# Starting expert 0 inside the drain of the attention pipeline: four early slots, unrolled experts, and a split shared with GpSimd

## The chip, the core and the metric

The kernel runs on one core of one Trainium2 chip, in one launch. The metric is the device time in microseconds (us). The kernel before takes 1063.76 us (median of 3 runs, 1062.62 to 1063.82).

A core has five engines with a queue of instructions each: TensorE (PE, matrix products into the PSUM banks), VectorE (DVE), ScalarE (ACT), GpSimd (POOL) and SyncE (SP, which issues most transfers). They meet only at semaphores. Transfers run on 16 shared DMA engines.

## The reference, cut to what matters

```python
x = layernorm(x + retention(x))                    # 32 sequences of 128 tokens, 256 channels
x = layernorm(x + cross_attention(x, ctx))         # causal, 16 heads
logits = x @ router_w.T                            # 8 experts, top 2 of them per token
h = gelu(x_e @ w_fc[e] + b_fc[e])                  # 256 -> 1024, expert by expert
y_e = h @ w_proj[e] + b_proj[e]                    # 1024 -> 256
x = layernorm(x + sum of y_e * share_e)
```

## The kernel before, in words

**Attention stage.** The 32 sequences go through a software pipeline. `step(k)` exists once on each engine and works on parts of the sequences k+1 to k-4: retention for k, the row maxima of attention for k-1, its values for k-2, second norm and router logits for k-3, top 2 and the place of each row for k-4. An engine takes these parts in the order in which the code writes them. `pick` finds the top 2, `put` counts and gives each token its row in the region of its expert, and on GpSimd `shares` works out the two weights of a token and `send` scatters its two rows into `sent_rows` in DRAM by indirect DMA. `filled` holds the next free row of each region.

**Drain.** After step 31 only the late parts are left. `step_drained` runs them on TensorE, with three filler products (`idle`, L625) ahead of each. When the last `put` is done, a chain of small VectorE instructions (L1112 to L1127) makes the table `tab_i`: slots per expert and the number of the first one. TensorE runs 64 filler products (`CHANGE_IDLE`) meanwhile.

**Expert stage.** The rows of an expert are taken in slots of 256. For each slot SP loads the rows, TensorE turns them (`turn_rows`, L673), ScalarE and VectorE make a high part and a low part of them (`xs_hi`, `xs_lo`), and TensorE runs 8 pieces `fc(j)` of 6 products (L699) and 8 pieces `proj(j)` of 6 products (L710); `proj` runs three pieces behind `fc`. For each piece ScalarE computes GELU twice (`h_hi` L903, `h_f` L909), and VectorE the difference `h_lo` (L1158). GpSimd adds the two halves of the weighted result to `residual_sum` (L1306). In the first slot of each expert the weights of the next are split as well: ScalarE makes seven of the eight high parts (`split_hi`, L837) and VectorE the eighth (`last_hi`, L1057) and all eight low parts (`split_lo`, L1062). Two sets of split weights take turns; `w_raw` is one buffer, loaded again (2 MB, L330 and L333) when `raw_split` says that it has been split.

Each engine runs the experts as a loop over three pairs and two more bodies written out. At the head of each body it loads the number of slots and the number of the first slot from `tab_i` into registers.

**Split of expert 0.** It is done in steps 28 to 31 (`SPLIT`, `SPLITS`), two of eight pieces a step.

**Last stage.** 8 blocks of 512 tokens are loaded, normalized and stored.

## Time and profile before

| | |
|---|---|
| median of 3 runs | 1063.76 us |
| profiled execution: its time, its span | 1062.52 us, 1060.7 us |
| steps 2 to 31 of the attention stage | 16.17 us each up to step 27, then 17.2 us |
| last attention product `att_values(31)` to first expert product | 551.5 to 580.1 us |
| expert products, 36 slots | 580.1 to 1025.1 us |
| last loads, norm, stores | 1025.1 to 1060.7 us |
| busy | PE 92%, DVE 61%, ACT 55%, POOL 34% of the span |
| granted TensorE clock | 0.979 of full speed on average |

How to read it: the busy share of an engine is an average over stages that are bound in different ways. In the expert stage what matters is the distance between the starts of slots; in the attention stage the distance between the starts of steps; and between the two stages the chain of waits. A row of the chain has its start, its length, the engine, what it writes and the line. "issue" is time in which the engine waited for nothing that the profile shows.

### The profile page before, as it was taken

The numbers are of one execution on the slowest core, as the hardware profiler recorded it, in microseconds if no ns is written. First come the engines' busy times: TensorE is split into PE (matmuls) and PEld (weight loads), VectorE is DVE, ScalarE is ACT, GpSimd is POOL, SyncE is SP. The second block draws the span as 40 slices with busy tenths as digits, with TensorE's granted clock in tenths as the row PEclk, the third lists the DMA queues.
The fourth block names the chain that finished last, engine by engine and source line by source line (L and its number), as shares of the span: only waits on it lengthen the run. The fifth ranks groups of instructions, "written<-read, shape, count | busy, mean of one in ns | idle before, by whom it ended". The sixth has DMA issues, their size and how long they took to land.

```text
span 1060.7 us, 31797 instructions
## 1 busy us (share of the span) xinstructions
PE 979.8 (92%) x11554; PEld 876.7 (83%) x11560; DVE 641.8 (61%) x1951; ACT 588.5 (55%) x1565; POOL 359.1 (34%) x599
## 2 busy tenths in 40 slices
PE   6999999999999999999887999999999999999960
PEld 4778888888888888888654999999999899999960
DVE  3467676676776676767743645565464655564436
ACT  3455555555655555556531656565565665565534
POOL 1124443444444444444433122222323222223223
PEclk9899999999999999999999999999999999999985
DMA  6001231111111111110032144422525342522227
GB/s 235 32 24 50 87 137 52 62 42 51 62 37 57 47 47 63 41 37 33 16 120 76 32 95 84 120 49 41 138 40 137 84 86 40 129 43 48 45 36 316
DMA packets 55831, 78.73 MB, mean 74 GB/s; under 512 B 5616, under 2 KB 44784, under 8 KB 55472
## 3 DMA queue, kind: packets, MB, share of 16 engines
q1 hardware_dynamic: 39984, 57.45, 16.9%
q0 software_dynamic: 13536, 18.16, 9.9%
q10 hardware_dynamic: 2208, 1.73, 0.6%
q8 instruction: 67, 1.10, 0.4%
q14 instruction: 36, 0.29, 0.1%
HBM read 51.04 MB, written 28.66 MB: 75 GB/s over the span
## 4 chain that ended last, share of the span: by engine, by line
PE 66%; DVE 15%; issue 6%; ACT 4%; POOL 4%; DMA 3%; ACTq 1%; DVEq 0%; POOLq 0%; SPq 0%
PE bank L699 17%; PE bank L710 16%; DVE row_max L945 7%; PE bank L437 5%; PE bank L552 3%; PE bank L452 3%; PE bank L427 3%; PE bank L597 3%; PE bank L505 3%; PE bank L477 3%; ACT h_f L909 2%; PE bank L583 2%; PE bank L472 2%; POOL grstd L1238 2%; DVE x_pre L976 1%
## 5 line engine op out<-in xcount | busy, mean ns | idle before, releaser
L903 ACT ACTIVATE h_hi<-bank,bfc_s 128x256 fp32r<-128x256 f32 x288 | 140.1, 487 | 175.0 <-PE bank L699 171.0
L1306 POOL DMA_INDIRECT residual_sum<-y_w,meta_i x72 | 117.6, 1634 | 340.9 <-DVE y_w L1182 330.0
L1158 DVE TENSOR_TENSOR h_lo<-h_f,h_hi 128x256 fp32r<-128x256 f32 x288 | 122.6, 426 | 176.6 <-ACT h_f L909 156.9
L699 PE MATMUL bank<-xs_hi,w_hi 128*128 128x256 f32 x576 | 166.4, 289 | 16.5 <-DVE xs_lo L1140 9.4
L699 PE MATMUL bank<-xs_lo,w_hi 128*128 128x256 f32 x576 | 162.7, 282 | 0.0
L710 PE MATMUL bank<-w_hi,h_lo 128*128 128x256 f32 x576 | 162.6, 282 | 0.0
L710 PE MATMUL bank<-w_hi,h_hi 128*128 128x256 f32 x576 | 162.5, 282 | 0.0
L699 PE MATMUL bank<-xs_hi,w_lo 128*128 128x256 f32 x576 | 161.2, 280 | 0.0
L710 PE MATMUL bank<-w_lo,h_hi 128*128 128x256 f32 x576 | 161.0, 280 | 0.0
L909 ACT ACTIVATE h_f<-bank,bfc_s 128x256 f32<-128x256 f32 x288 | 140.1, 487 | 0.0
L699 PEld LDWEIGHTS bank<-xs_hi,w_hi 128*128 128x128 f32 x576 | 108.4, 188 | 19.5 <-issue 19.5
L710 PEld LDWEIGHTS bank<-w_hi,h_hi 128*128 128x128 f32 x576 | 108.3, 188 | 0.7
L699 PEld LDWEIGHTS bank<-xs_lo,w_hi 128*128 128x128 f32 x576 | 108.5, 188 | 0.0
L699 PEld LDWEIGHTS bank<-xs_hi,w_lo 128*128 128x128 f32 x576 | 108.3, 188 | 0.0
L710 PEld LDWEIGHTS bank<-w_lo,h_hi 128*128 128x128 f32 x576 | 108.3, 188 | 0.0
L710 PEld LDWEIGHTS bank<-w_hi,h_lo 128*128 128x128 f32 x576 | 108.2, 188 | 0.0
L805 ACT ACTIVATE att_p<-bank 128x512 f32<-128x512 f32 x128 | 69.2, 599 | 28.7 <-PE bank L561 28.7
L940 DVE TENSOR_TENSOR ret_p<-bank,decay 128x512 f32<-128x512 f32 x128 | 79.2, 681 | 7.9 <-PE bank L452 7.9
L945 DVE TENSOR_REDUCE row_max<-bank 128x4 f32<-128x512 f32 x128 | 78.9, 679 | 2.5 <-PE bank L530 2.5
L1269 POOL DMA_INDIRECT sent_rows<-x_row,pos x64 | 64.3, 1005 | 18.3 <-issue 14.5
L415 PE MATMUL bank<-xcT,wqk_s 128*128 128x128 f32 x512 | 65.6, 281 | 0.8 <-DMA wqk_s<-in_w_qkv 0.8
L415 PEld LDWEIGHTS bank<-xcT,wqk_s 128*128 128x128 f32 x512 | 59.6, 191 | 7.0 <-issue 5.8
(170 smaller groups left out, 1985.1 us busy)
## 6 DMA issues: line engine op xcount, KB each, us to landing
rows<-sent_rows SPq DMA_DIRECT2D x37, 258.0 KB
xcT<-in_turned SPq DMA_DIRECT2D x32, 256.0 KB, 2.9
w_raw<-in_w_fc SPq DMA_DIRECT2D x8, 1024.0 KB
w_raw<-in_w_proj SPq DMA_DIRECT2D x8, 1024.0 KB
x_t<-in_x SPq DMA_DIRECT2D x32, 128.0 KB, 2.7
residual_sum<-x_row SPq DMA_DIRECT2D x32, 128.0 KB, 1.8
last_in<-residual_sum SPq DMA_DIRECT2D x8, 512.0 KB, 7.5
result<-last_out SPq DMA_DIRECT2D x8, 512.0 KB, 2.7
```

The source lines that it names most:

```text
L415: last = mm(ps_prep[:, m * P:(m + 1) * P], wqk_s[:, k, m * P:(m + 1) * P], xcT[c.r][:, 0, k, :], start=(k == 0), stop=(k == NCH - 1))
L437: last = mm(ps_prep[:, i * C:(i + 1) * C], xcT[c.r][:, i, k, :], w[:, k, :], start=(k == 0), stop=(k == NCH - 1))
L699: last = mm(ps_h[j % 4][:, 0:SLOT], w[:, at:at + P], v[:, k, :], start=(n == 0), stop=(n == 3 * NCH - 1))
L710: last = mm(ps_out[half][:, 0:C], v[j % 4][:, cols], w[:, at:at + C], start=(j == 0 and n == 0), stop=(j == HC - 1 and n == 2))
L805: A(att_p[:, r, :], ps_s[r][:, :], ACT.Exp, scale=SCALE).then_inc(s["att_exp"], 1)
L903: A(h_hi[j % 4][:, :], ps_h[j % 4][:, 0:SLOT], ACT.Gelu_apprx_tanh, bias=bias)
L909: A(h_f[j % 2][:, :], ps_h[j % 4][:, 0:SLOT], ACT.Gelu_apprx_tanh, bias=bias)\
L940: V.tensor_tensor(ret_p[:, r, :], ps_s[r][:, :], decay[:, r, :], ALU.mult)\
L945: V.reduce_max(row_max[:, r, 0:HPT], ps_s[r][:, :].rearrange("p (h s) -> p h s", s=T), AX.X)\
L1158: V.tensor_tensor(h_lo[j % 4][:, :], h_f[j % 2][:, :], h_hi[j % 4][:, :].bitcast(f32), ALU.subtract).then_inc(s["h_split"], 1)
L1269: G.indirect_dma_start(sent_flat, bass.IndirectOffsetOnAxis(pos[c.r][:, k:k + 1], 0), x2_row[c.r][k][:, :], None).then_inc(s_sent[c.r], 16)
L1306: G.indirect_dma_start(total, bass.IndirectOffsetOnAxis(meta_i[:, half:half + 1], 0), y_w[:, half, :], None, compute_op=ALU.add)\
```

## The change

1. **Early slots.** The first 27 sequences (`EARLY_SEQ`) send their rows for expert 0 to the first rows of `sent_rows`; 4 slots (`EARLY`) of 256 rows of it are computed straight behind `att_values(31)`. The remaining parts of the drain (`rank_out`, `rank_last`, `last_norms`, `last_places`, `copies_last`) and the table are written between the pieces of slots 0 and 1. `put` sets the counter of expert 0 to at least 1024 after sequence 26, so that the region behind holds the rest. These 1024 rows are filled with padding at the very start, by four transfers on SP's queue that GpSimd waits for (`early_padded`) before its first work.
2. **Experts written out.** `experts` is a Python loop over 8 experts with fixed numbers. Each engine loads the 8 slot counts once, TensorE in slot 2 and ScalarE and VectorE in slot 3, and adds registers after that.
3. **GpSimd's share.** `ON_POOL = (1, 3, 5)`: three of eight low parts of the next weights are made by GpSimd. VectorE still waits for all eight (`w_ready`) at the end of the first slot.
4. **Split of expert 0** in steps 21 to 28, one piece a step, and the load of the weights of expert 1 from step 29.
5. **`gap_exp`** leaves ScalarE. GpSimd computes the exponential as a power, as the first link of `shares`.
6. The two halves of the result share one PSUM bank; `rows` goes to another bank. `CHANGE_IDLE` and the advance load of the GELU table (L880) are gone.

```diff
-SPLIT = B - 4
-SPLITS = 2
+SPLIT = B - 11
+SPLITS = 1
-CHANGE_IDLE = 64
+EARLY = 4
+EARLY_SEQ = 27
+ON_POOL = (1, 3, 5)
...
-            with eng.Fori(0, E // 2 - 1) as pair:
-                for k in range(2):
-                    body(2 * pair + k, k, True, True)
-            body(E - 2, 0, True, False)
-            body(E - 1, 1, False, False)
+            g = EARLY
+            for e in range(E):
+                body(e, e % 2, slots[e], g, e + 1 < E, e + 2 < E)
+                g = g + slots[e]
...
+                if k == B - 1:                      # SP
+                    for r in range(4):
+                        sp.wait_ge(s_sent[r], 32 * len(range(r, EARLY_SEQ, 4)))
+                    early_rows(0)
                 run(store_total, At(k - 3))
+                if k == 0:
+                    for g in range(EARLY):
+                        sp.dma_start(sent_flat[g * SLOT:(g + 1) * SLOT, :].rearrange("(h p) c -> p h c", p=P),
+                                     pad_row).then_inc(s["early_padded"], 16)
...
+            def rank_out(j):                        # TensorE, beside slot 0
+                if j == 0:
+                    logits(At(B - 2))
+                if j == 1:
+                    o_turn(At(B - 1))
+                if j == 3:
+                    att_back(At(B - 1))
+                if j == 4:
+                    att_proj(At(B - 1))
+                    rank(At(B - 2))
+                if j == 8:
+                    x2_turn(At(B - 1))
+                if j == 10:
+                    logits(At(B - 1))
...
+            slot(0, 0, rank_out)
+            slot(1, 0, rank_last)
+            slot(2, 0, count_next)
+            for g in range(3, EARLY):
+                slot(g, 0)
...
-            act.wait_ge(s["gap_exp"], B)
-            A(gelu_warm[:, :], half_neg[:, 0:1], ACT.Gelu_apprx_tanh)
+            def copies_last(j):                     # ScalarE, beside slot 0
+                if j == 3:
+                    att_back_out(At(B - 1))
+                if j == 6:
+                    x2_T_out(At(B - 1))
+                    x2_again(At(B - 1))
...
+            def last_norms(j):                      # VectorE, beside slot 0
+                if j == 0:
+                    lg_out(At(B - 2))
+                if j == 1:
+                    att_norm(At(B - 1))
+                if j == 2:
+                    pick(At(B - 2))
+                if j == 4:
+                    ln2_stats(At(B - 1))
+                    put(At(B - 2))
+                if j == 5:
+                    ln2_norm(At(B - 1))
...
-                pool.wait_ge(s["gap_exp"], c.n + 1)
+                pool.wait_ge(s["gap_done"], c.n + 1)
+                ch.link(G.tensor_tensor(gap_e[:, :], base_e, gap[:, :], ALU.pow))
...
+            pool.wait_ge(s["early_padded"], 16 * EARLY)
             for half in range(HALVES):
                 G.dma_start(total[N_TOK + half * P:N_TOK + (half + 1) * P, :], pad_row[:, half, 0:C])
+            slots = []
+            steps(step)
+            drain()
...
+                if has_next:                        # GpSimd, head of each expert
+                    for j in ON_POOL:
+                        split_lo(e + 1, 1 - par, j)
```

What the edits do to the order of the queues, at four places.

TensorE between the stages, before: L625 is filler, L605 `x2_turn`, L611 `logits`, L619 and L620 `rank`, L673 `turn_rows` of the first slot.

```order
L620 MATMUL bank<-hot_b,bits 128x8
L625 MATMUL bank<-bits 128x512 x3
L605 MATMUL bank<-small,x_row_0 128x128 x2
L625 MATMUL bank<-bits 128x512 x3
L611 MATMUL bank<-rt_s,x2T 128x8 x2
L625 MATMUL bank<-bits 128x512 x3
L619 MATMUL bank<-hot_b,bits 128x8
L620 MATMUL bank<-hot_b,bits 128x8
L625 MATMUL bank<-bits 128x512 x64
L673 MATMUL bank<-small,rows 128x128 x4
```

After, in the same place: L605 is now `att_values(31)`, L704 `fc`, L643 `logits`, L615 `o_turn`, L657 filler.

```order
L637 MATMUL bank<-small,x_row_0 128x128 x2
L657 MATMUL bank<-bits 128x512 x3
L605 MATMUL bank<-att_p,v_att 32x128 x16
L704 MATMUL bank<-xs_hi,w_hi 128x256
L704 MATMUL bank<-xs_lo,w_hi 128x256
L704 MATMUL bank<-xs_hi,w_lo 128x256
L704 MATMUL bank<-xs_hi,w_hi 128x256
L704 MATMUL bank<-xs_lo,w_hi 128x256
L704 MATMUL bank<-xs_hi,w_lo 128x256
L643 MATMUL bank<-rt_s,x2T 128x8 x2
L704 MATMUL bank<-xs_hi,w_hi 128x256
L704 MATMUL bank<-xs_lo,w_hi 128x256
L704 MATMUL bank<-xs_hi,w_lo 128x256
L704 MATMUL bank<-xs_hi,w_hi 128x256
L704 MATMUL bank<-xs_lo,w_hi 128x256
L704 MATMUL bank<-xs_hi,w_lo 128x256
L615 MATMUL bank<-small,att_o 128x128 x4
L704 MATMUL bank<-xs_hi,w_hi 128x256
```

The first product of expert 0 stands directly behind the last product of attention, and the late parts of the drain stand between its pieces. The 64 filler products are gone.

ScalarE in the same place, before: L829 is `gap_exp`, L823 `x2_again`, L880 the advance load of the GELU table, L889 `xs_high(0)`.

```order
L818 ACTIVATE x2T<-bank 128x256 [waits x2_T]
L829 ACTIVATE gap_e<-gap 128x1 [waits shared,gap_done]
L823 ACTIVATE x_row_1<-x_row_0 128x256 [waits x2_done]
L829 ACTIVATE gap_e<-gap 128x1 [waits shared,gap_done]
L880 ACT_TABLE_LOAD
L880 ACTIVATE gelu_warm<-small 128x1 [waits gap_exp]
L889 ACTIVATE xs_hi<-bank 128x512 [waits consts_expert,tab_ready,rows_turned]
```

After: L888 is `att_exp(31)`, L901 `x2_T_out`, L892 `o_out`, L906 `x2_again`, L962 and L968 the two GELU outputs of slot 0.

```order
L888 ACTIVATE att_p<-bank 128x512 [waits att_scores] x4
L901 ACTIVATE x2T<-bank 128x256 [waits x2_T]
L892 ACTIVATE att_o<-bank 128x512 [waits att_done]
L906 ACTIVATE x_row_1<-x_row_0 128x256 [waits x2_done]
L962 ACT_TABLE_LOAD [waits consts_expert,fc_done]
L962 ACTIVATE h_hi<-bank,bfc_s 128x256
L968 ACTIVATE h_f<-bank,bfc_s 128x256 [waits h_split]
```

The table for GELU is now loaded behind the wait for the first `fc` of slot 0 (`fc_done`), and `o_out(31)` and `x2_again(30)` stand ahead of it.

GpSimd at the start of the program, before: L1228 makes `xb` of sequence 0, L1235 to L1238 its `grstd`.

```order
L1220 UNCONDITIONAL_BRANCH [waits barrier_Pool_Activation_PE_DVE_SP_gather]
L1228 ISA
L1228 TENSOR_TENSOR xb<-x_t,gnb 128x256 [waits zeroed,got_late,loaded0,got_small,got_gn]
L1235 TENSOR_TENSOR gmsq<-gm 128x1 [waits gn_moments]
L1236 TENSOR_TENSOR gvar<-gm,gmsq 128x1 [waits gn_chain]
L1237 TENSOR_TENSOR gvar<-gvar,small 128x1 [waits gn_chain]
L1238 TENSOR_TENSOR grstd<-gvar,small 128x1 [waits gn_chain]
```

After: L1476 fills the padding rows behind `residual_sum` (formerly L1288, at the end of the attention stage), L1375 makes `xb`.

```order
L1367 UNCONDITIONAL_BRANCH [waits barrier_Pool_Activation_PE_DVE_SP_gather]
L1476 DMA residual_sum<-in_small_c 128x256 [waits zeroed,got_late,early_padded,got_small,got_gn]
L1476 DMA residual_sum<-in_small_c 128x256
L1375 ISA
L1375 TENSOR_TENSOR xb<-x_t,gnb 128x256 [waits loaded0]
L1382 TENSOR_TENSOR gmsq<-gm 128x1 [waits gn_moments]
L1383 TENSOR_TENSOR gvar<-gm,gmsq 128x1 [waits gn_chain]
L1384 TENSOR_TENSOR gvar<-gvar,small 128x1 [waits gn_chain]
L1385 TENSOR_TENSOR grstd<-gvar,small 128x1 [waits gn_chain]
```

Two transfers and the wait for `early_padded` stand ahead of the first `xb` now.

SyncE after, at the end of expert 0: L398 is the loop over slots, L403 loads rows, L337 and L340 load the weights of expert 2, L299 and L300 pad the region of expert 2.

```order
L398 UNCONDITIONAL_BRANCH
L398 ISA
L403 ISA
L403 DMA rows<-sent_rows 128x2x258
L398 REGISTER_ALU
L398 COMPARE_AND_BRANCH
L337 DMA w_raw<-in_w_fc 128x2x1024
L340 DMA w_raw<-in_w_proj 128x8x256
L299 TENSOR_LOAD tab_i
L299 ISA x2
L300 ISA
L300 DMA sent_rows<-in_small_c 128x2x258
L398 UNCONDITIONAL_BRANCH
L398 ISA
L403 ISA
L403 DMA rows<-sent_rows 128x2x258
```

The order of these transfers is that of before; but the first loop now runs twice for expert 0 instead of six times, so the rows of expert 1's first slot stand behind the weights of expert 2 one slot after these are asked for.

## Rows read from the trace of the kernel before

**Rows 1.** Chain of waits, slots (start, length, engine, tile, line, count).

```profile
605.48 2.84 PE bank L699 x24
...
617.29 2.84 PE bank L699 x24
...
653.67 1.00 PE bank L699 x6
...
667.02 3.12 PE bank L699 x24
...
673.69 0.44 PE bank L673 x4
```

**Rows 2.** Chain of waits, attention steps and last split.

```profile
460.87 1.73 PE bank L437 x8
...
477.04 1.73 PE bank L437 x8
...
494.25 1.73 PE bank L437 x8
...
528.27 1.04 ACT w_hi L837 x2
```

**Rows 3.** Windows (length, PE, PEld, DVE, ACT, POOL busy, clock, DMA share, GB/s).

```profile
530.00:534.00 4.00, 4.00 (x20) 3.36 (x23) 1.95 (x11) 0.55 (x2) 1.52 (x2) 0.51 0.20 70
```

**Rows 4.** Chain of waits, from attention to the first expert.

```profile
550.47 1.01 PE bank L573 x32
...
555.57 0.97 PE bank L597 x4
...
560.10 0.31 PE bank L605 x2
...
569.87 4.46 DMA sent_rows<-x_row,pos
...
580.06 2.42 PE bank L699 x18
```

**Rows 5.** Timeline of ScalarE at the change of stages.

```profile
562.95 1.28 ACT L880 ACT_TABLE_LOAD   x1
```

**Rows 6.** Waits of TensorE after 580 us.

```profile
PE bank L699 <- issue: 7.2, 7, 1.4
```

**Rows 7.** Timeline of GpSimd at the start.

```profile
20.50 0.72 POOL L1228 TENSOR_TENSOR xb<-x_t,gnb 128x256 f32<-128x256 f32 x1 [20.03 <-DMA rt_s<-in_router_t]
```

**Rows 8.** Windows at the start, and over a load of weights.

```profile
16.00:18.00 2.00, 2.00 (x35) 1.71 (x24) 0.04 (x1) 1.12 (x5) 0.00 (x0) 1.00 1.06 372
18.00:20.00 2.00, 2.00 (x18) 1.84 (x16) 0.61 (x2) 0.10 (x1) 0.00 (x0) 1.00 0.40 120
630.00:641.00 11.00, 11.00 (x96) 11.00 (x95) 4.94 (x14) 6.81 (x17) 3.31 (x2) 1.00 0.93 262
```

**Rows 9.** DMA issues of SyncE (KB each, us to landing).

```profile
sent_rows<-in_small_c SPq DMA_DIRECT2D x8, 258.0 KB, 8.1
```

**Rows 10.** GpSimd issues on `residual_sum` (ns min/median/max).

```profile
L1288 POOL DMA_DIRECT2D residual_sum<-in_small_c x2: 561/590/620, 570.8 to 571.4; - x2
```

**Rows 11.** Timeline of SyncE in the first slots.

```profile
630.01 0.37 SPq L330 DMA_DIRECT2D w_raw<-in_w_fc  x1
...
633.33 0.66 SPq L293 DMA_DIRECT2D sent_rows<-in_small_c  x1
```

**Rows 12.** Single lines of VectorE and GpSimd (ns min/median/max, first and last).

```profile
L976 DVE SCALAR_TENSOR_TENSOR x_pre<-y_c,grstd,xb x32: 484/485/485, 22.6 to 522.0; 128x256 f32<-128x256 f32 x32
...
L1238 POOL TENSOR_TENSOR grstd<-gvar,small x32: 548/561/567, 22.0 to 521.4; 128x1 f32<-128x1 f32 x32
...
L1246 POOL TENSOR_TENSOR x_row<-gap_s,small x32: 548/691/692, 82.7 to 566.2; 128x1 f32<-128x1 f32 x32
...
L1261 POOL TENSOR_TENSOR x_bo<-x,bo_s x32: 722/730/733, 25.2 to 527.9; 128x256 f32<-128x256 f32 x32
...
L1062 DVE TENSOR_TENSOR w_lo<-w_raw,w_hi x64: 681/693/761, 477.8 to 939.4; 128x512 fp32r<-128x512 f32 x64
```

More of the change, by code:

```diff
@@ L276, in steps @@
                 between()
-            for k in range(B + DRAIN):
+            for k in range(B):
                 step(k)
@@ L351, in _ @@
             steps(step)
+            for k in range(B, B + 3):
+                step(k)
             sp.wait_ge(s["counts_ready"], 1)
@@ L651, in step @@
                 run(o_turn, At(k - 2))
-            def step_drained(k):
-                for stage, back in ((att_back, 3), (att_proj, 3), (att_scores, 2), (rank, 4), (x2_turn, 3),
-                                    (att_values, 2), (logits, 3), (o_turn, 2)):
-                    if At(k - back).exists():
-                        idle(DRAIN_IDLE)
-                        stage(At(k - back))
             def between():
@@ L665, in _ @@
             idle(START_IDLE, y_sq[:, 0:TW * 2].bitcast(bf16), y_sq[:, :].bitcast(bf16))
-            steps(step, between)
             def turn_rows(g):
@@ L728, in _ @@
-            experts(pe, expert)
+                with pe.Fori(0, n_slots) as i:
+                    slot(before + i, par)
+            experts(expert, slots)
         @block.scalar
@@ new lines, in _, with expert @@
+            act.wait_ge(s["got_small"], 16)
+            steps(step, between)
+            drain()
+            act.wait_ge(s["consts_expert"], 16 * CONSTS_EXPERT)
+            act.sem_inc(s["h_done"], EVER)
+            slot(0, 0, None, copies_last)
+            for g in range(1, EARLY - 1):
+                slot(g, 0)
+            act.wait_ge(s["tab_ready"], 1)
+            slots = []
+            slot(EARLY - 1, 0, None, lambda j: slots.append(count(act, j)))
+            def expert(e, par, n_slots, before, has_next, has_after):
+                slot(before, e, (e + 1, 1 - par) if has_next else None)
@@ L917, in expert @@
                 with act.If(n_slots > 1):
                     with act.Fori(1, n_slots) as i:
-                        slot(before + i, False)
-            experts(act, expert)
+                        slot(before + i, e)
+            experts(expert, slots)
             for b in range(NLAST):
@@ new lines, in _, with expert @@
+            steps(step)
+            drain()
+            dve.wait_ge(s["consts_expert"], 16 * CONSTS_EXPERT)
+            slot(0, 0, None, last_norms)
+            slot(1, 0, None, last_places)
+            for g in range(2, EARLY - 1):
+                slot(g, 0)
+            dve.wait_ge(s["tab_ready"], 1)
+            slots = []
+            slot(EARLY - 1, 0, None, lambda j: slots.append(count(dve, j)))
+            def expert(e, par, n_slots, before, has_next, has_after):
+                slot(before, e, (e + 1, 1 - par) if has_next else None)
@@ L1186, in expert @@
                 with dve.If(n_slots > 1):
                     with dve.Fori(1, n_slots) as i:
-                        slot(before + i, False)
-            experts(dve, expert)
+                        slot(before + i, e)
+            experts(expert, slots)
             def last_stats(b):
@@ L1289, in _ @@
                     .then_inc(s_added[half], 16 * EVER)
+            slots = []
+            steps(step)
+            drain()
             for r in range(4):
```

474 lines of the change are left out of this document (284 added, 190 removed).

## The prediction, made before the changed kernel was run

> **What bounds the kernel now.** I read the chain of waits first, because it says for each stage which engine's end is waited for. In the expert stage it is TensorE: a plain slot runs from 605.48 to 617.29, 11.81 us of products [rows 1]. The first slot of an expert takes 667.02 - 653.67 = 13.35 us, since ScalarE and VectorE also split the next weights there and the next slot's low part comes late [rows 1]. At each of the 7 changes of expert TensorE waits about 1 us more for nothing but its own register loads: 7.2 us in all [rows 6]. In the attention stage a step takes 477.04 - 460.87 = 16.17 us, and 494.25 - 477.04 = 17.21 us where expert 0's weights are split [rows 2]. Its period is not TensorE's work but a loop: products, `grstd` on GpSimd, `x_pre` on VectorE, the row maxima, products again. Between the stages the reader is to see a long chain in which TensorE has nothing but filler: attention's last product ends at 550.47 + 1.01 = 551.48, then come the projection, the norm and the turn (560.10), the last send lands (569.87 + 4.46), and the first expert product starts at 580.06 [rows 4]. That is 28.6 us.
>
> **The sum, part by part**, against the profiled execution (1062.52 us; the median of the runs is 1.2 above it).
>
> *Handover, -28.6.* The number of slots stays: by the inputs expert 0 gets 1300 rows, 1094 of them from the first 27 sequences, so 4 early slots are full and 2 follow; 6 before, 4 + 2 after. So the whole of 551.48 to 580.06 goes, and what was computed in it comes back inside slots 0 and 1.
>
> *What stands before the first GELU, +1.1.* In the order of after `o_out(31)` and `x2_again(30)` stand ahead of slot 0 on ScalarE. `x2_again` takes some 0.4 us and `o_out` is waited for behind `att_values(31)`; I take 1.1 for the start of the GELU chain.
>
> *Slot 0, +7.0.* Products that moved in: two logits, `o_turn`, `att_back`, `att_proj` (555.57), one `rank`, `x2_turn` (0.31 us [rows 4]), some 3.3 us, an estimate from the lengths of such products. Stalls: the GELU table (1.28 us [rows 5]) is now loaded behind the wait for the first `fc`, so it lies on the path; `o_turn`, `rank` and `proj(7)` each wait for a piece of VectorE or ScalarE that is queued behind the GELUs and differences of the slot, together about 2.5. So 3.3 + 1.3 + 2.4 = 7.0. From below 4.6 (only products and table); from above 12, if each of the five late parts (turn, back, projection, norm, turn) waits its own way through two busy engines, at 1 to 2 us each.
>
> *Slots 1 and 2, +1.4.* One `rank` and a table of 2.6 us of VectorE, which has slack in a plain slot (its own busy share is under half, 4.94 of 11 us [rows 8]): +0.4. Slot 2 has the 8 register loads on TensorE: one change of expert costs 1.0 for two loads and the branch [rows 6]; eight loads spread over pieces, +1.0 (0 to 4).
>
> *The drain's first part, -2.0.* The chain has 1.04 us of ScalarE's split in step 31 [rows 2], which is gone, and behind it the clock dips: 0.51 of full speed, half of the 2.4 GHz, from 530 to 534, when TensorE had waited for that split [rows 3]. I take 1.0 of the dip's 2 us.
>
> *The split spread, -2.2.* Four steps of two pieces cost 4 x (17.21 - 16.17) = 4.2. Now eight steps have one piece: ScalarE and VectorE each have one less operation of 0.7 us [rows 12] in the loop's slack, which I put at 0.25 a step: 2.0 instead of 4.2 (0 to 4.2).
>
> *Experts written out, -3.2.* Seven waits of 1.0 [rows 6]; the loop branch inside an expert stays and one jump remains, about 0.5 each: 7.2 to 4.0 (0.7 to 7).
>
> *The start, +5.5.* This is the added wait with the largest price. GpSimd's queue now begins with the wait for four transfers of 258 KB, and behind that wait stand two transfers of its own and then `xb(0)`; `x_pre(0)` on VectorE waits for `xb(0)`, and the whole pipeline behind it. Before, `xb(0)` started at 20.50, held by the last constant that it needs [rows 7]. In this stretch the DMA engines are full: share 1.06 from 16 to 18 us and 0.40 from 18 to 20 [rows 8]; so the pads can't be moved beside the constants, only behind them. One costs, by 2882 KB in 11 us at share 0.93 [rows 8], 258 / 282 = 0.9 us of all engines, say 1.1; four, 4.4. They finish at about 18.8 + 4.4 + 1.5 of landing = 24.7, and GpSimd issues its two transfers at 0.59 us each [rows 10]: `xb(0)` starts at 25.9, +5.4. From below 1.2 (the two issues only, the pads fully hidden); from above 9, a pad by itself takes 8.1 us from issue to landing [rows 9].
>
> *Expert 0 with two slots, +6.0.* SyncE's queue has, in order, the rows of slot 5, the weights of expert 2 (2 MB), the pad of expert 2, the rows of slot 6 (the order of after). The weights wait for the split of the raw ones, done about 12.5 us into slot 4. Before, expert 0 had six slots, and this load was issued at 630.01 beside its fifth [rows 11], its pad 3.3 us later; nothing waited. Now the rows of slot 6 are issued about 15 us after slot 4's start, behind 2 MB and 258 KB on the same queue: at 262 GB/s [rows 8] 2048 + 258 KB are 9 us, so they land near 25.5. TensorE needs them for `turn_rows(6)` in slot 5, at 673.69 - 653.67 = 20.0 [rows 1]. The stall is 5.5 us, and a wait of this length may cost the clock that rows 3 show, 0.5 more. From below 0 (rows pass beside the weights), from above 8 (with the full dip).
>
> *GpSimd's three low parts, +2.0.* A GpSimd operation on 128x256 takes 0.73, the VectorE one on 128x512 0.69 [rows 12]; so one piece on GpSimd is an estimated 1.45. VectorE is relieved of 3 x 0.69, but at the end of a first slot it is late because ScalarE's last GELU is late, not for its own work; no gain. The wait that this adds: VectorE waits for all eight parts (`w_ready`) at j = 7, and behind that stand the low part of the next rows, for which TensorE waits, and the bias. GpSimd should be done about 2 us before. I put +0.3 for each of 7 experts for operations side by side (0 to 0.6 each: `x_row` takes 0.548 at least and 0.691 in the median [rows 12], so operations on these two engines do stretch one another).
>
> *`gap_exp`.* GpSimd's power is the first link of `shares`; as a 128x1 operation with a power it costs 0.56 like `grstd` [rows 12], on an engine with 34% of work, and its chain has a whole step. +0.2 with the rest.
>
> Sum: -28.6 + 1.1 + 7.0 + 1.4 - 2.0 - 2.2 - 3.2 + 5.4 + 6.0 + 2.0 + 0.2 = -12.9. 1062.5 - 12.9 = 1049.6; with half of the 1.2 to the median, **1050**.
>
> **The rivals.**
>
> *A. The two added queues cost nothing* (the start 1.2 instead of 5.4, the rows of slot 6 not late): 1050 - 4.2 - 6.0 = 1040, and less with a smaller slot 0. For it: the DMA engines are idle from 20 to 22 us, and the transfers have 16 engines. Against: both stand in one queue in order, and the wait on GpSimd is ahead of all its work. Chance 0.15.
>
> *B. Slot 0 is much longer* (12 instead of 7), because five late parts follow each other through engines that also do GELU: 1055 to 1058. For it: the same chain took from 551.5 to 569.9 when these engines were free [rows 4]. Against: slot 1 takes part of it. Chance 0.10.
>
> *C. The loop of the steps grows: slower than before.* Its place is between `grstd` and `x_pre`. `pow` of `gap` is the next thing in GpSimd's queue behind `grstd`, reads SBUF, lasts 0.56 us, and `x_pre` (484 ns, two SBUF inputs, on the loop) starts 0.04 to 0.08 us after `grstd` ends. If an operation of GpSimd that holds SBUF keeps VectorE out to its end, `x_pre` starts up to 0.5 us late in 28 steps: 14 us, and each of the three low parts costs VectorE 0.6 instead of 0.3 per expert (+2). That gives 1050 + 14 + 2 = 1066. It decides the sign from (1063.8 - 1050 - 2) / 28 = 0.42 us a step. Against it: `gap_s` of GpSimd stands beside `x_pre` now, and `x_pre` is 484 to 485 ns in all 32 steps; what is longer is GpSimd's `x_row`, 0.69 against 0.55 [rows 12]. So GpSimd seems to be the one held, at least where VectorE comes first. Chance 0.07.
>
> The Trainium skill ("SBUF — State Buffer", section "Who interferes with whom") has this rule: a VectorE instruction with two SBUF inputs contends with a GpSimd instruction that reads SBUF, through a shared pair of ports which whoever issues first holds for the whole instruction. By that rule case C is how it would go, since `pow` issues first; the trace agrees with it in that `x_row` is longer beside `x_pre`, and has no row in which a long GpSimd operation came first.
>
> *D. The change doesn't do what it says:* the 27 sequences do not fill 1024 rows, and a slot of padding (+11.8) is computed. 1094 against 1024: chance 0.01.
>
> **How the numbers follow.** The forecast (1044 to 1056) has 0.65, A 0.15, B 0.10, C 0.07, D and the rest 0.03. The range 1039 to 1058 takes in A and most of B, and leaves C, D and the far ends of the bounds, some 0.15. About 0.2% or 2.1 us is what a measurement of this kernel can tell from no change: faster needs 1061.6 or less. That holds for the forecast, A and B: 0.90. Same 0.03, slower (C, and D with B) 0.07.
>
> **What the profile after would show.** Right, if: `xb(0)` starts near 26; steps are still 16.2 apart up to the first split and 16.4 in steps 21 to 28; the first `fc` stands directly behind `att_values(31)`; slot 0 lasts 19; the GELU table load is on the chain inside it; `turn_rows(6)` waits some 5 us for a transfer; the issue wait at changes of expert halves; first slots stay 13.4 to 13.7. Wrong, if `x_pre` starts 0.3 us or more behind `grstd`, if `xb(0)` starts before 23 or after 29, if slot 0 exceeds 24, or if VectorE waits for GpSimd at `w_ready`.

## The result, and the profile after

The changed kernel takes 1058.44 us (median of 14 runs) against 1063.28 us of the kernel before: ratio of 0.9958, 95% interval 0.9945 to 0.9972. It is faster by 4.8 us; 1050 was forecast, with a range of 1039 to 1058. One of the 14 runs, of 1116.65 us at a granted clock of 0.924, was in a slower state of the chip and is not in the ratio.

The chain of waits of the changed kernel has these rows at the start and at the change of stages (start, length, engine, tile, line, count); they answer to [rows 1, 2, 4 and 7].

```profile
12.19 12.41 DMA sent_rows<-in_small_c
...
25.28 1.37 POOL residual_sum L1476 x2
26.75 0.74 POOL xb L1375
...
28.86 0.49 DVE x_pre L1077
```

```profile
530.08 0.50 DVE x_pre L1077
...
556.56 1.06 PE bank L605 x32
557.80 0.95 PE bank L704 x6
...
631.41 7.55 DMA rows<-sent_rows
639.00 0.66 PE bank L690 x4
...
644.64 0.72 PE bank L704 x6
...
659.40 3.13 PE bank L704 x24
```


The first rows are the added wait: the last of SyncE's pads lands at 24.6, two transfers of GpSimd follow, and `xb(0)` starts at 26.75. In the second block `att_values(31)` ends at 557.6 and the first expert product starts 0.2 us later: the gap of 28.6 us is gone. But at 631.41 a load of rows takes 7.55 us, and the first slot of expert 1, from 644.64 to 659.40, lasts 14.8 us (13.35 in the kernel before).

TensorE's waits in the expert stage (line waited with, releaser: us in total, times, longest), as [rows 6]:

```profile
PE bank L717 <- DVE h_lo L1248: 11.5, 8, 1.5
PE bank L704 <- DVE xs_lo L1218: 7.6, 7, 1.1
PE bank L690 <- DMA rows<-sent_rows: 3.2, 1, 3.2
PE bank L615 <- DVE lg L1125: 1.9, 1, 1.9
```


The 7.2 us of issue are no longer there. In their place stand 11.5 us for `h_lo`, a wait that the kernel before did not have.

Where the time went, from the starts of `x_pre` (L976, now L1077) of each step and of `xs_lo` (L1140, now L1218) of each slot, in both traces. A plain slot is 11.81.

| stretch | before | after | difference | forecast |
|---|---|---|---|---|
| `x_pre(0)` starts | 22.59 | 28.86 | +6.3 | +5.4 |
| steps 0 and 1 | 27.47 | 28.36 | +0.9 | 0 |
| steps 2 to 30 (split) | 471.97 | 472.86 | +0.9 | -2.2 |
| `x_pre(31)` to the end of attention | 29.45 | 27.53 | -1.9 | -2.0 |
| to the first expert product | 28.58 | 0.19 | -28.4 | -28.6 |
| slots 0 to 3, beyond plain slots | | | +9.6 | +9.5 |
| second slot behind the early ones | | 14.97 | +3.4 | +6.0 |
| changes of expert | 7.2 | 0 | -7.2 | -3.2 |
| 7 first slots | 97.0 | 107.3 | +10.3 | +2.0 |
| 15 other slots of odd experts | 11.81 | 11.95 | +2.0 | 0 |
| last stage | 37.00 | 37.26 | +0.3 | 0 |

The 97.0 are the sum of the first slots before (103.2) without the six waits of about 1.03 us at their start. The rows give -3.8; the spans differ by -4.1. The rows of the start hold some scatter: seven traces with the same code up to step 3 have `x_pre(0)` at 27.8 to 28.9 and 26.8 to 28.4 us for steps 0 and 1. Slots 0 to 3: from the first product to `xs_lo(1)` 19.26, in a plain slot 10.45, so +8.8; then +0.6, +0.3, -0.1.

### The profile page after: what moved, and what is told of

The parts are those of the page before. It is cut to its first block, busy times and chain, and to the rows that moved or that the text cites. A ratio compares the mean times of both kernels' runs of the same rounds, so it can differ in the third digit from the quotient of the medians.

```text
span 1056.6 us, 31053 instructions
## 1 busy us (share of the span) xinstructions
PE 965.9 (91%) x11474; PEld 873.5 (83%) x11474; DVE 648.2 (61%) x1931; ACT 587.5 (56%) x1531; POOL 399.0 (38%) x651
## 4 chain that ended last, share of the span: by engine, by line
PE 67%; DVE 16%; issue 6%; POOL 4%; ACT 3%; DMA 3%; SPq 1%; ACTq 0%; DVEq 0%; POOLq 0%
PE bank L717 16%; PE bank L704 16%; DVE row_max L1046 7%; PE bank L469 5%; PE bank L584 3%; PE bank L484 3%; PE bank L459 3%; PE bank L537 3%; PE bank L629 3%; PE bank L509 3%; PE bank L615 2%; PE bank L504 2%; POOL grstd L1385 2%; DVE x_pre L1077 1%; ACT h_f L968 1%
## 5 line engine op out<-in xcount | busy, mean ns | idle before, releaser
L1248 DVE TENSOR_TENSOR h_lo<-h_f,h_hi 128x256 fp32r<-128x256 f32 x288 | 124.9, 436 | 183.4 <-ACT h_f L968 183.0
L962 ACT ACTIVATE h_hi<-bank,bfc_s 128x256 fp32r<-128x256 f32 x288 | 139.0, 483 | 172.7 <-PE bank L704 170.7
L717 PE MATMUL bank<-w_hi,h_hi 128*128 128x256 f32 x576 | 164.3, 285 | 11.5 <-DVE h_lo L1248 11.5
L704 PE MATMUL bank<-xs_hi,w_hi 128*128 128x256 f32 x576 | 167.3, 290 | 7.8 <-DVE xs_lo L1218 7.6
L704 PE MATMUL bank<-xs_lo,w_hi 128*128 128x256 f32 x576 | 163.1, 283 | 0.0
L704 PE MATMUL bank<-xs_hi,w_lo 128*128 128x256 f32 x576 | 162.8, 283 | 0.0
L968 ACT ACTIVATE h_f<-bank,bfc_s 128x256 f32<-128x256 f32 x288 | 138.0, 479 | 11.5 <-DVE h_lo L1248 11.5
L717 PEld LDWEIGHTS bank<-w_hi,h_hi 128*128 128x128 f32 x576 | 109.6, 190 | 13.6 <-DVE h_lo L1248 13.1
L704 PEld LDWEIGHTS bank<-xs_hi,w_hi 128*128 128x128 f32 x576 | 109.8, 191 | 9.4 <-issue 9.4
L704 PEld LDWEIGHTS bank<-xs_lo,w_hi 128*128 128x128 f32 x576 | 110.0, 191 | 0.0
L704 PEld LDWEIGHTS bank<-xs_hi,w_lo 128*128 128x128 f32 x576 | 109.8, 191 | 0.0
L888 ACT ACTIVATE att_p<-bank 128x512 f32<-128x512 f32 x128 | 69.3, 599 | 27.6 <-PE bank L593 27.6
```

The costliest lines, as they stand in the source:

```text
L704: last = mm(ps_h[j % 4][:, 0:SLOT], w[:, at:at + P], v[:, k, :], start=(n == 0), stop=(n == 3 * NCH - 1))
L717: last = mm(ps_out[half], v[j % 4][:, cols], w[:, at:at + C], start=(j == 0 and n == 0 and half == 0), stop=(j == HC - 1 and n == 2 and ha ...
L888: A(att_p[:, r, :], ps_s[r][:, :], ACT.Exp, scale=SCALE).then_inc(s["att_exp"], 1)
L962: A(h_hi[j % 4][:, :], ps_h[j % 4][:, 0:SLOT], ACT.Gelu_apprx_tanh, bias=bias)
L968: A(h_f[j % 2][:, :], ps_h[j % 4][:, 0:SLOT], ACT.Gelu_apprx_tanh, bias=bias)\
L1248: V.tensor_tensor(h_lo[j % 4][:, :], h_f[j % 2][:, :], h_hi[j % 4][:, :].bitcast(f32), ALU.subtract).then_inc(s["h_split"], 1)
```

## The experiments

"Less" is against the 1058.44 of the changed kernel, and the ratios are to the kernel before. Edits are to the changed kernel unless said otherwise. Experiments 1, 3, 4 and 5 ran on one chip, 2, 6, 7 and 8 on a second, 9, 10 and 12 on a third and 11 on a fourth; the kernel before took 1062.8 to 1063.7 us on each.

### 1. No low part on GpSimd

```diff
-ON_POOL = (1, 3, 5)
+ON_POOL = ()
```

> All eight low parts go back to VectorE; all else as in the changed kernel. Theory (T1, GpSimd's 128x512 subtractions hold VectorE's out until they end; one w_lo of VectorE lasts 3.87 us beside two of them, 0.69 alone): every w_lo of VectorE is 0.69 to 0.76 us again, the waits of the proj products for h_lo (11.5 us) go, the 7 first slots fall from 15.4 to about 13.8 between the low parts of the rows, total 9 to 12 us less than the changed kernel. Rival (R1, VectorE and GpSimd share bandwidth evenly and the longer first slots come from the written-out code or the new place of the tiles): first slots stay near 15, total within 3 us of the changed kernel.

Measured 1046.40 us (ratio to the kernel before 0.9841, 0.9826 to 0.9856), 12.0 less. The seven first slots add up to 95.0 instead of 107.3. What happens with GpSimd's share is on the timelines of VectorE and GpSimd in the first slot of expert 1 of the changed kernel (start, length, engine, line, operation, tiles):

```profile
646.86 0.69 DVE L1165 TENSOR_TENSOR w_lo<-w_raw,w_hi 128x512 fp32r<-128x512 f32 x1
...
648.84 0.42 DVE L1248 TENSOR_TENSOR h_lo<-h_f,h_hi 128x256 fp32r<-128x256 f32 x1 [0.82 <-ACT h_f L968]
649.37 3.87 DVE L1165 TENSOR_TENSOR w_lo<-w_raw,w_hi 128x512 fp32r<-128x512 f32 x1
653.16 0.75 DVE L1248 TENSOR_TENSOR h_lo<-h_f,h_hi 128x256 fp32r<-128x256 f32 x2
653.83 0.68 DVE L1165 TENSOR_TENSOR w_lo<-w_raw,w_hi 128x512 fp32r<-128x512 f32 x1
...
655.45 0.89 DVE L1248 TENSOR_TENSOR h_lo<-h_f,h_hi 128x256 fp32r<-128x256 f32 x1 [0.60 <-ACT h_f L968]
```

```profile
648.58 1.57 POOL L1427 DMA_INDIRECT residual_sum<-y_w,meta_i  x1 [0.30 <-issue]
649.58 3.10 POOL L1436 TENSOR_TENSOR w_lo<-w_raw,w_hi 128x512 fp32r<-128x512 f32 x2
654.76 1.30 POOL L1436 TENSOR_TENSOR w_lo<-w_raw,w_hi 128x512 fp32r<-128x512 f32 x1 [2.08 <-ACT w_hi L914]
```


VectorE's `w_lo` of 0.69 us lasts 3.87, from 649.37 to 653.24, and GpSimd's two lie inside it, 649.58 to 652.68. `h_lo` is queued behind, so ScalarE and TensorE wait too. The lengths nearly add up: 0.69 and 3.10 are 3.79. Beside GpSimd's third (654.76) an `h_lo` of 0.42 lasts 0.89. Duration of all `w_lo` of VectorE (ns min/median/max), with three, with none, and GpSimd's with one:

```profile
L1165 DVE TENSOR_TENSOR w_lo<-w_raw,w_hi x43: 676/692/3952, 371.9 to 935.5; 128x512 fp32r<-128x512 f32 x43
```

```profile
L1165 DVE TENSOR_TENSOR w_lo<-w_raw,w_hi x64: 691/692/695, 371.0 to 923.7; 128x512 fp32r<-128x512 f32 x64
```

```profile
L1436 POOL TENSOR_TENSOR w_lo<-w_raw,w_hi x7: 1868/1879/1894, 621.4 to 921.9; 128x512 fp32r<-128x512 f32 x7
```


T1 holds: without GpSimd's share no `w_lo` of VectorE is over 695 ns, and the first slots fall to 13.6 on average. R1 falls. The second slot behind the early ones takes 16.5 us here instead of 15.0: TensorE waits the same 3.2 us for the rows, and behind the wait its clock is at half for about 3 us, as in the traces of experiments 4, 5 and 7 and not in that of the changed kernel.

### 2. One low part on GpSimd

```diff
-ON_POOL = (1, 3, 5)
+ON_POOL = (1,)
```

> GpSimd makes one low part instead of three, VectorE seven. Theory (T6, the one who streams 128x512 from SBUF on GpSimd keeps VectorE's two-input operation out until its end, so the price goes by how much of VectorE's work falls beside it): one w_lo of VectorE per expert lasts 1.5 to 2.3 us, the others 0.69, first slots 13.6 to 14.4, total 7 to 11 us less than the changed kernel. Rival (R6, an even share of bandwidth over the stretch in which both work): no w_lo of VectorE over 1.4 us, first slots near 14.2, total about 8 less.

Measured 1052.07 us (0.9903, 0.9886 to 0.9921), 6.4 less: first slots 14.2, and in each one `w_lo` of VectorE of 2.6 to 2.75 us. T6 had 1.5 to 2.3 and a total of 7 to 11 less, and is missed by both; its first slots of 13.6 to 14.4 came. R6 had none over 1.4 and falls. In expert 1:

```profile
649.77 2.64 DVE L1165 TENSOR_TENSOR w_lo<-w_raw,w_hi 128x512 fp32r<-128x512 f32 x1
649.98 1.88 POOL L1436 TENSOR_TENSOR w_lo<-w_raw,w_hi 128x512 fp32r<-128x512 f32 x1
```

`w_lo` lasts from 649.77 to 652.41 and GpSimd's from 649.98 to 651.86: VectorE's begins first and ends 0.55 us behind, as beside two, and again the lengths nearly add up (0.69 and 1.88 are 2.57). One piece costs 0.6 us an expert in the first slots (99.1 in all), three cost 1.75.

### 3. Tiles 32 bytes further on

```diff
+        sb("gap64", [P, 8])
```

> Only 32 bytes of unused SBUF behind `small`, so that every later tile begins where its address divided by 64 leaves what it left before (0 instead of 32). Theory (T2, the place of the second set of split weights makes the 32 products with w_lo of a plain slot slower, 0.120 instead of 0.115 us apart, in odd experts alone): plain slots of odd experts fall from 11.95 to 11.81, total 2 us less. Rival (R2, it isn't the place modulo 64 but the tile's neighbourhood, or the code of the odd experts): odd plain slots stay 11.95, total unchanged within 0.5 us.

Measured 1057.89 us (0.9954, 0.9936 to 0.9972), the same within the spread. Plain slots of odd experts stay 11.95, of even ones 11.82. T2 falls.

### 4. The wait for the pads in step 3

```diff
-            pool.wait_ge(s["early_padded"], 16 * EARLY)
-            for half in range(HALVES): ...   # both transfers move too
...
+                if k == 3:
+                    pool.wait_ge(s["early_padded"], 16 * EARLY)
+                    for half in range(HALVES): ...
```

> GpSimd waits for the four early pads, and fills the padding rows of the sum, in step 3 ahead of the first send, no longer ahead of the first xb. Theory (T3, the wait and the two transfers of GpSimd cost the start 6.3 us and step 0 another 0.8): xb(0) starts at 20.5 to 21.5 and x_pre(0) at 22.6 to 23.5, total 5 to 7 us less. Rival (R3, SyncE's pads delay the loads of the constants themselves, whatever GpSimd waits for): x_pre(0) at 27 or later, total within 2 us of the changed kernel.

Measured 1055.31 us (0.9916, 0.9896 to 0.9937), 3.1 less. `xb(0)` starts at 21.97 and `x_pre(0)` at 24.07, 4.8 earlier; the rest of the 6.3 is SyncE's pads beside the constants, since with them in step 1 (experiment 8) `xb(0)` starts at 20.40, as before. R3 had `x_pre(0)` at 27 or later and falls; T3 had it at 22.6 to 23.5 and a total of 5 to 7 less, and both are missed a little. The 4.8 and the rest are rough, since the same start moves by about 1 us between traces: 25.65 to 26.76 for `xb(0)` in those with the code of the changed kernel there, 20.28 to 21.47 in those with that of experiment 8. The total shows less than the 4.8: TensorE is at half clock for 10 us in the drain here (experiment 7), and from `x_pre(31)` to `xs_lo(1)` the trace has 49.2 us, the changed kernel 47.0.

### 5. Expert 0 split in steps 28 to 31

```diff
-SPLIT = B - 11
-SPLITS = 1
+SPLIT = B - 4
+SPLITS = 2
```

> Expert 0's weights are split in steps 28 to 31 again, two pieces a step. Theory (T4, a piece costs a step 0.45 us, two pieces 1.05; eight single pieces 3.8 in all, four pairs 4.2 plus the clock at half speed behind the last of them): 1 to 3 us more than the changed kernel, steps 21 to 27 16.17 apart. Rival (R4, the spread brings nothing, since the last step's wait in the drain is hidden now): within 0.5 us of the changed kernel.

Measured 1056.67 us (0.9939, 0.9924 to 0.9954), 1.8 less, against T4, which had 1 to 3 more, and outside R4's 0.5. Only 0.7 of it is the split: from `x_pre(2)` to `x_pre(31)` the trace has 472.13 instead of 472.86. Seven steps of 16.61 and one of 16.86 are worse than three of 17.2 and one that the drain hides: from `x_pre(31)` to the first expert product both have 27.7. The rest is scatter: `x_pre(2)` comes 2.3 us earlier here, and half clock behind the wait for the rows gives some of it back.

### 6. Rows of slot 6 ahead of the weights

```diff
+                if e == 1:                   # SyncE
+                    slot_rows(0)
+                    sp.wait_ge(s["raw_split"], 2)
+                    load_weights(2)
...
-                if has_after:
+                if has_after and e > 0:
```

> SyncE issues the rows of slot 6 (first of expert 1) ahead of the weights of expert 2, all else as in the changed kernel. Theory (T5, those rows land 11 us after their issue since 2 MB and a pad are ahead of them in the queue, and TensorE waits 3.2 us in slot 5): no wait of L690 for rows any more, the low part of slot 6 follows that of slot 5 after 11.6 us, not 15.0; total 3 us less. Rival (R5, the wait moves on: the weights of expert 2 now land late for the first slot of expert 1, ScalarE waits for them): slot 5 is short but slot 6 longer by as much, total within 1 us.

Measured 1057.09 us (0.9941, 0.9926 to 0.9956), 1.4 less. In the trace T5 holds in what it says of the slots: the slot takes 11.57 instead of 14.97, and the one after it 15.29 as ever, so R5 falls. (The rows of the changed kernel landed 7.55 us after their issue, not 11.) But the total is not 3 us less: from `x_pre(31)` to `xs_lo(1)` this trace has 51.8 us, the changed kernel 47.0. One cause is the clock (experiment 7). The other is a wait of VectorE ahead of `row_max(31)` for which the profile names no releaser in the core:

```profile
DVE row_max L1055 <- remote: 4.3, 1, 4.3
```

It is not this edit's doing. `row_max(31)` waits for `max_scores` alone, which only TensorE raises, with its last products on the scores: these end at 543.36 as the profile models them, and VectorE starts at 544.88. The profile seems to lose the name because the signal came late. The trace of experiment 7, from the same chip and without this edit, has nearly the same wait under TensorE's name:

```profile
DVE row_max L1047 <- PE bank L562: 3.8, 1, 3.8
```

Its first expert product starts 32.55 us after `x_pre(31)`, the one here 32.54. Experiment 2, on that chip too, has 3.8 and 32.6. The changed kernel (whose chip is not on record) and experiments 1, 3, 4 and 5 wait 2.1 to 2.8 us at this place; all eight other traces, from three other chips, wait 3.8 to 4.3, with the edit or without it. Where a trace has half clock for about 3 us only, the first expert product comes 27.3 to 27.7 us after `x_pre(31)` in the first group and 30.8 to 31.0 in the second (8, 10 and 11). So some 3 us go with the chip or the time of the run. Why TensorE's signal comes later there stays open. A difference of 1 to 3 us between totals of experiments from different chips shows nothing by itself.

### 7. The GELU table ahead of slot 0

```diff
+                A(gelu_warm[:, :], half_neg[:, 0:1], ACT.Gelu_apprx_tanh)
                 x2_T_out(At(B - 2))
```

> ScalarE runs one dummy GELU on one column behind att_exp(31), which loads the GELU table before slot 0. Theory (T7, the table load of 1.28 us behind the wait for the first fc is on the path of slot 0): h_hi(0) starts 0.1 to 0.2 us after fc_done instead of 1.4, xs_lo(1) follows the first fc after 18.0 instead of 19.3, total 1.3 us less. Rival (R7, slot 0 is set by its late drain parts on VectorE, which wait anyway): slot 0 shorter by less than 0.4 us; or the table load delays o_out(31) and with it att_norm(31), which gives the time back.

Measured 1058.57 us (0.9962, 0.9947 to 0.9977), no difference. The trace supports T7: from the first product to `xs_lo(1)` 16.48 us, against 17.75 to 17.78 in the traces of experiments 2, 3 and 4 (and 19.3 where the clock fell in slot 0). All five later kernels with the edit have 16.5. R7's slot shorter by less than 0.4 us falls. The total doesn't show the 1.3 us; between chips and clocks it can't. Windows of 4 us (length, busy time of the five engines, granted clock, DMA share, GB/s) in the changed kernel and in that of experiment 6:

```profile
534.00:538.00 4.00, 3.85 (x16) 2.36 (x16) 1.36 (x5) 2.63 (x8) 2.31 (x3) 0.61 0.00 0
562.00:566.00 4.00, 4.00 (x24) 4.00 (x23) 1.93 (x10) 1.68 (x4) 0.38 (x1) 0.57 0.02 4
```

```profile
542.00:546.00 4.00, 4.00 (x54) 3.40 (x53) 1.12 (x2) 0.00 (x0) 1.96 (x2) 0.50 0.19 66
546.00:550.00 4.00, 2.97 (x30) 1.91 (x24) 1.95 (x6) 2.25 (x6) 0.00 (x0) 0.50 0.01 4
```


TensorE is at 1.2 GHz (0.50; a dip, below) at three places of the drain and slot 0 (elsewhere once, 19 us after `x_pre(31)` in experiment 12), and which of them a trace has differs:

- 3 to 6 us after `x_pre(31)`, for about 3 us, behind a wait of TensorE of 1.8 us for `row_max`: in all these traces but that of experiment 12, which has the same wait;
- 14 us after it, for about 10 us, behind waits for `hot_b` and `filled` of 0.2 and 0.6 us: in experiments 2, 4, 6, 7 and 9, not in the others, which have the same two waits;
- in slot 0, for about 3 us, behind a wait of 1.9 us for the logits: in the changed kernel and in experiments 1, 5 and 6, not in 2, 3 and 4.

For the same products in this stretch, on one chip, the time from `x_pre(31)` to `xs_lo(1)` is 45.1 us with the first dip alone (experiment 3), 47.0 with the first and the third (experiments 1 and 5; the changed kernel too), and 49.2 with the first and the second (experiment 4). That is a spread of 4 us in which single gains of 1 us are lost.

### 8. All of them

Experiments 1, 4, 5, 6 and 7 together, and SyncE's pads one step later:

```diff
-                if k == 0:                   # SyncE
+                if k == 1:
                     for g in range(EARLY):
                         sp.dma_start(sent_flat[g * SLOT:(g + 1) * SLOT, :] ...
```

> All edits that follow from the runs so far: no low part on GpSimd, the wait for the early pads and GpSimd's two transfers in step 3, SyncE's pads in step 1 instead of step 0, two pieces a step in steps 28 to 31, rows of slot 6 ahead of the weights of expert 2, the GELU table before slot 0. By the sizes measured or expected one by one (12.0, 5 to 6, 0.7, 3.2 to 4.7, 1.3 less than the changed kernel): 1034 to 1036 us, xb(0) at 20.5. Rival: part of these gains share one wait, total above 1039.

Measured 1035.28 us (0.9748, 0.9732 to 0.9765), 23.2 less, within the 1034 to 1036 expected. The totals measured one by one add up to 18.2 only (12.0, 3.1, 1.8, 1.4 and -0.1); the sizes in the traces come to more. The slot that waited for rows takes 11.56 us, 5.0 less than the 16.5 of experiment 1, where the half clock behind the wait is in it. And `xb(0)` starts at 20.40. Part of the agreement is luck, since this chip adds some 3 us in the drain (experiment 6).

### 9. VectorE's low part one step later

```diff
-                if SPLIT <= k < SPLIT + HC // SPLITS:         # VectorE
+                if SPLIT < k <= SPLIT + HC // SPLITS:
                     for j in range(SPLITS):
-                        split_lo(0, 0, SPLITS * (k - SPLIT) + j)
+                        split_lo(0, 0, SPLITS * (k - 1 - SPLIT) + j)
```

(on 8, with one piece a step in steps 21 to 28; SyncE loads the weights of expert 1 one step later too)

> The combined kernel, but with expert 0's split in steps 21 to 28, one piece a step, and VectorE's low part of a piece taken one step after ScalarE's high part. Theory (T9, a step with one piece takes 16.61 because VectorE waits 1.2 us for ScalarE's high part ahead of ret_decay): VectorE no longer waits there, steps 22 to 29 are 16.17 to 16.25 apart, total 2 to 3 us less than the combined kernel (three steps of 17.2 gone). Rival (R9, the price is ScalarE's own 0.65 us in the step, which holds the copies that TensorE waits for): steps stay 16.6, total 0.7 us more than the combined kernel.

Measured 1033.47 us (0.9717, 0.9695 to 0.9739), 1.8 less than 8 and 0.6 less than experiment 10 on the same chip; neither total is clear of the spread. In the trace all steps up to step 30 take 16.16 to 16.20 us, and from `x_pre(2)` to `x_pre(31)` it has 468.88 us, 3.3 less than 8. On VectorE's timeline the low part in the changed kernel waits, and `ret_p`, which TensorE needs, stands behind it; one step later it does not wait:

```profile
469.99 0.40 DVE L1092 TENSOR_SCALAR x<-x_pre,l1mv,l1rstd 128x256 f32<-128x256 f32 x1
471.62 0.69 DVE L1165 TENSOR_TENSOR w_lo<-w_raw,w_hi 128x512 fp32r<-128x512 f32 x1 [1.22 <-ACT w_hi L914]
472.23 2.48 DVE L1041 TENSOR_TENSOR ret_p<-bank,decay 128x512 f32<-128x512 f32 x4
```

```profile
459.34 0.40 DVE L1102 TENSOR_SCALAR x<-x_pre,l1mv,l1rstd 128x256 f32<-128x256 f32 x1
459.66 0.68 DVE L1175 TENSOR_TENSOR w_lo<-w_raw,w_hi 128x512 fp32r<-128x512 f32 x1
460.26 2.48 DVE L1051 TENSOR_TENSOR ret_p<-bank,decay 128x512 f32<-128x512 f32 x4
```


T9 holds for the steps, and R9 falls; T9's total of 2 to 3 less is missed by a little.

### 10 and 11. The second pair of weight tiles swapped; the other tiles ahead of the first pair

```diff
-        w_hi = [w_hi0, sb("w_hi1", [P, WROW], f32r)]       # 10, on 8
         w_lo = [w_lo0, sb("w_lo1", [P, WROW], f32r)]
+        w_hi = [w_hi0, sb("w_hi1", [P, WROW], f32r)]
```

> The combined kernel with the second pair of weight tiles in the other order in SBUF (low part first). Theory (T10, the products of the low part are further apart when that tile lies where w_lo1 lay): plain slots of odd experts 11.81, total 2 us less. Rival (R10, it follows the experts, whatever the order of the two tiles, so its cause is the neighbourhood of both or the code): 11.95 stays. A third way: the two thirds of the products that use the high part become slower instead, 12.0 or more.

```diff
+        rows = sb("rows", [P, HALVES, ROW])                # 11, on 9; so too the tiles down to y_w
+...
         w_raw = sb("w_raw", [P, WROW])
         w_hi0 = sb("w_hi0", [P, WROW], f32r)
         w_lo0 = sb("w_lo0", [P, WROW], f32r)
-        rows = sb("rows", [P, HALVES, ROW])
-...
```

> The kernel with the low part one step later, and with rows, the h, xs and y tiles in SBUF ahead of w_raw and the first pair of weight tiles (they then lie together, as in the kernel before; the second pair stays where it is). Theory (T12, plain slots of odd experts are slower since their weight tiles lie behind the tiles of h and xs): they fall to 11.81 or all experts become alike, total up to 2 us less. Rival (R12, only the place of the second pair itself counts, or the code): odd 11.95, even 11.81, total unchanged within 1 us.

Experiment 10 measured 1034.05 us (0.9729, 0.9716 to 0.9742) and odd plain slots of 11.95, even 11.82: T10 falls and R10 holds. Experiment 11 measured 1033.47 us (0.9716, 0.9692 to 0.9741), and now the even experts have 11.95 as well. That is T12's second outcome, all experts alike, but with the longer time; R12 falls. The total is that of 9, though the longer slots add some 2 us, since this trace has no dip of 10 us in the drain and that of 9 has one. Only the place of tiles was changed there: the first pair of weights moved up by 20,608 bytes, the others down to make room, the second pair stayed. So the 0.14 us follow the place of tiles in SBUF, not the code of the odd experts. Mean durations of the products with `w_lo` and `w_hi` (us busy, mean ns) in 11, to be compared with 282 (first line) and 280 (second line) in the kernel before:

```profile
L711 PE MATMUL bank<-xs_lo,w_hi 128*128 128x256 f32 x576 | 162.8, 283 | 0.0
L711 PE MATMUL bank<-xs_hi,w_lo 128*128 128x256 f32 x576 | 162.8, 283 | 0.0
```


Which property of the place it is stays open.

### 12. Six fillers in the drain

```diff
-DRAIN_IDLE = 3
+DRAIN_IDLE = 6
```

(on 8)

> The combined kernel with six filler products in place of three ahead of each late part of the drain. Theory (T11, the stretches at 1.2 GHz between 526 and 553 us, 3 to 14 us long and at another place in each run, follow TensorE's waits in the drain; more filler closes them): fewer such stretches, median 1 to 3 us less, spread between runs smaller. Rival (R11, the fillers stand ahead of parts that others wait for and cost 0.65 us for three each): 1 to 4 us more than the combined kernel.

Measured 1039.02 us (0.9777, 0.9764 to 0.9791), 3.7 more than 8. In the drain its trace has only one dip, of about 3 us between 538 and 544, but the first expert product starts 33.5 us after `x_pre(31)` instead of 30.9 (30.8 in experiment 10, on the same chip). T11 falls and R11 holds: the filler costs more than the clock gives back.

## Why the prediction was wrong

- **Handover, first part of the drain, early slots** (-28.6, -2.0, +9.5): right, each within 0.2 us, though with luck: of the 9.6 some 1.5 are a stretch at 1.2 GHz in slot 0 that I had not put there, and the register loads cost 0.3 instead of 1.0. The -1.9 of the drain's first part goes by which dips a trace has: the same stretch takes 27.1 us in experiment 3 and 31.2 in experiment 4.
- **GpSimd's three low parts** (+2.0): this is the step that failed. Experiment 1 measured 12.0 us. I took the price, 0.3 us an expert, from rows of small operations that lie side by side, set VectorE's relief at nothing, and counted on GpSimd finishing in time for `w_ready`. It did; what was late was VectorE itself. Beside GpSimd's 128x512 subtraction VectorE's hardly progresses: 0.69 becomes 3.87 beside two and 2.64 beside one, about its own length and theirs. `h_lo` is queued behind it, and ScalarE and TensorE wait for that: 1.75 us an expert. The prediction's sign for this, first slots that stay at 13.4 to 13.7, failed; its other one, VectorE waiting for GpSimd at `w_ready`, never came.
- **Rival C** had this mechanism at another place. There it did not come: GpSimd's power of 128x1 at 414.45 lies beside `x_pre`, and both keep their lengths (`x_pre` takes 483 to 486 ns in all 32 steps, against 484 to 485 in [rows 12]):

```profile
413.93 0.56 POOL L1385 TENSOR_TENSOR grstd<-gvar,small 128x1 f32<-128x1 f32 x1
414.45 0.56 POOL L1392 TENSOR_TENSOR gap_e<-small,gap 128x1 f32<-128x1 f32 x1
```

```profile
414.53 0.48 DVE L1077 SCALAR_TENSOR_TENSOR x_pre<-y_c,grstd,xb 128x256 f32<-128x256 f32 x1 [0.81 <-POOL grstd L1385]
```


The Trainium skill ("SBUF — State Buffer", section "Who interferes with whom") says that a VectorE instruction with two SBUF inputs contends with a GpSimd instruction that reads SBUF. The trace agrees for the two subtractions (3.87 against 0.69 us), and in that `ret_p`, which takes one operand from PSUM, stays at 0.68 us beside GpSimd's `x_bo` of 0.73. The first line is the length of all `ret_p` (ns min/median/max), the other two are one step in which `x_bo` lies inside the four of them:

```profile
L1041 DVE TENSOR_TENSOR ret_p<-bank,decay x128: 678/682/692, 12.6 to 521.8; 128x512 f32<-128x512 f32 x128
```

```profile
305.92 2.48 DVE L1041 TENSOR_TENSOR ret_p<-bank,decay 128x512 f32<-128x512 f32 x4
306.08 0.73 POOL L1409 TENSOR_TENSOR x_bo<-x,bo_s 128x256 f32<-128x256 f32 x1 [1.54 <-DVE x L1092]
```


Two things it does not bear out. The section says of the two-port modes that "Whoever issues first gets the shared pair for the whole instruction", and I took that for this case too, where it does not hold: here VectorE's started 0.21 us ahead of GpSimd's and ended 0.56 behind it. And GpSimd's power held nothing up. I had given the rule a chance of 0.07 and priced it at `x_pre`. For the 21 subtractions, which read 512 columns instead of one, it stood in that case with 2 us more (0.6 instead of 0.3 us an expert), where the runs show 1.75 us an expert.
- **Split spread** (-2.2, measured +0.9): the cost of a piece was not its length in slack, but the wait of VectorE for ScalarE's half: 0.45 a step with one piece, and nothing once the low part comes a step later (experiment 9).
- **Start** (+5.4 in the sum, 5.5 at the head of its paragraph; measured +6.3, and +0.9 in the two steps behind): the mechanism was right, and experiment 4 with 8 gives its two parts, about 4.8 for GpSimd's wait and 1.6 for the transfers. The 0.9 is no more than the scatter between traces.
- **Two slots of expert 0** (+6.0, measured +3.4): right in kind, the size partly luck. TensorE wanted the rows 21.3 us into slot 4, not 20.0, since the slot was itself longer, and they were there after 24.5 (639.0), not 25.5: asked for 2 us later than forecast (16.9, not 15) and under way for 3 us less (7.55, not 10.5). Experiment 1 shows which term was off: without GpSimd's share they are asked for after 15.2 us and wanted after 19.5, nearly as forecast, and land 7.5 later. The forecast counted the whole 2 MB from the issue of the rows, and the weights had been issued 3 us before.
- **Experts written out** (-3.2, measured -7.2): the whole wait went. Nothing of the branch is left on TensorE's path.
- **Odd experts** (+2.0): not in the prediction at all.

Of the 8.4 us by which 1050 was missed, GpSimd's share gives 10, the split 3, the start 2 and the tiles 2; the changes of expert and the shorter stall give back 4 and 2.6, and the first slots without GpSimd were 2 shorter than before (95.0 against 97.0), which no run explains.

## What to carry to other kernels

A streaming two-input operation moved to GpSimd is not free when VectorE has such operations at the same time: ask what VectorE does in that microsecond, not how busy it is. An engine that is the second of a pair of steps (high part, low part) should take its half one period later. A wait put at the head of an engine's queue delays all of its work at the start of the program: put it ahead of the first instruction that needs it.

## What the runs showed of the hardware

- GpSimd 128x512 beside VectorE 128x512, both with two operands in SBUF: VectorE's 0.69 becomes 2.6 to 2.75 us beside one and 3.9 beside two, though VectorE's starts first in all 14 cases; GpSimd's takes 1.28 to 1.90.
- The same products take 11.81 or 11.95 us a slot by the place of the weight tiles in SBUF.
- TensorE's granted clock falls to half for about 3 or 10 us at up to three places of the drain and slot 0, behind waits of 0.6 to 1.9 us; the same waits come without the fall in other traces. Between kernels with the same instructions there, on one chip, this moves the time by up to 4 us.
- The same drain takes some 3 us more in traces from three chips than in those from a fourth; the kernel before took the same on all four.
- Two loads of 1 MB and one of 258 KB ahead in the queue make a load of 258 KB land after 7.6 us; DMA share 0.95 from 629 to 639 us.
